# Three edits around the last layer's node stage: an earlier start for interleaved extra work, five norm groups ahead of the copies, and sums added on GpSimd

## The chip, the core and the metric

The kernel runs on one core of one Trainium2 chip. The metric is the device time of one execution in microseconds (us); for a kernel that was run several times it is the median.

## What is computed

Four graph layers over 3125 nodes with 128 features and 100,000 edges, all in fp32. Each layer is h = relu(layernorm(x)), x = x + layer(h). The layers are an edge MLP (with a residual of its own inside), a graph attention with 4 heads, a second attention with 8 heads and a bias, and a relational layer with 16 relations. Cut to the part at hand:

```python
h = relu(layernorm(x));  x = x + attention2(h, edges, W, a_left, a_right, bias)   # third layer
h = relu(layernorm(x))                                                            # fourth layer
weights = einsum('rb,bio->rio', coefficients, bases)      # 16 relation matrices
out = h @ w_self.T
out = out.at[src].add(h[dst] @ weights[edge_type])        # one term an edge
x = x + out
```

## The kernel before, in words

Nodes lie in 25 bins of 128 (the last one partly filled); a tile [128, 25, 128] holds x as `g.X`. Edges are sorted and cut into blocks of 512 (4 tiles of 128): 196 main blocks (numbers 0 to 195) and 12 extra ones (196 to 207), 208 in all; the extra blocks, and block 195, have 2 real tiles instead of 4. A stage is one hardware block: every engine runs its own instruction list, written out in full, and waits only where the text says `wait_ge`. Between stages all engines meet at a barrier.

**The attention stage** (`attention_sum`, third layer) goes over the 208 blocks in a software pipeline. GpSimd issues one gather DMA a tile (806 of them, line 1105, `att_row`). VectorE's list is made by `unrolled`: step k does `make_hot` of block k (L2352), `score` of block k-3 (L2362, waits for the gather), `message` of block k-4 (L2369, L2371) and `add_sum` of block k-6 (L1482, waits for TensorE's sum, L2340; TensorE starts the sum of block j once block j-2 is added and the message of j is there), and then takes one item of **extra work** with `next(extra, None)`. Steps run from 0 to 213; the extra work is taken from step `first` = `UNROLL` = 16 on, and what is left after step 213 runs behind the loop. The extra work is a chain of three generators: `add_bias` (9 items: the layer's bias into X), `merged_rows` (133 items: a merge sort of the edge words; its exchanges wait for DMAs that SyncE issues) and `relation_weights` (60 items of one 128x512 instruction, L360 and L366: the 16 relation matrices into `g.wall`), together 202 items.

**The relation stage** (`relation`, fourth layer) begins after the barrier. Its node part: the sums of the attention layer, divided by their denominators, are added to X; X is normed; H, its transpose `ht`, and 25 x 4 products of 128x512 (`product`, L1718) with `g.wall` make a table in HBM (`tables`, 25 writes of 1 MB, L1614). The norm (`Norm`) works in nine groups of three bins, `THREE`:

- VectorE: `residual` (L887: TMP = sums x 1/denominator, three instructions; L891: X += TMP, one 128x384 instruction), `scan` (bn_stats L897, bn_aggr L900), `scales` (L913, L914, waits for ScalarE's square root).
- ScalarE: `deviation` (L907, square root) and `apply` (L922, H, three instructions), put together in `scaled(n)`: deviation of group n, then apply of group n-1. Before the loop over bins it does `scaled(0)` to `scaled(2)`, with `keep_three` (L945, copies a transposed group from PSUM) after n = 1; then for each bin a: the copies of the bin's product banks into `stage` (L1672; from bin 4 on VectorE takes two of the four, L1810), and then `scaled(2a+3)`, `scaled(2a+4)` and, for a = 1, 4, 7..., `keep_three` of the next group.
- TensorE: `turn_three` (L937, transposes of a group) and the four products of a bin; product (a, part) waits until the copy of (a-1, part) has emptied its bank; bin 3n waits for `keep_three` of group n.
- SyncE: for each bin a write of `stage` to the table once the bin's copies are done; ahead of the writes of bins 1, 2 and 4 a third of H each to `tabh` (L1611), which wait for 3, 6 and 9 groups of `apply`. As the queue is in order, the last of them also waits for the copies of bin 3.
- GpSimd: waits for `s_node_i` and for the three writes to `tabh`; then 64 **early gathers** from `tabh` (L1640, 16 blocks), of which the last 16 (from block 12 on) go into the room of H and wait for the last transposes (`gp.wait_ge(s_t, len(THREE))`); then waits for all table writes; then the 742 gathers of the remaining 192 blocks (L1650), from the table into a ring of 16 blocks, which TensorE sums (L1756). Five output instructions on VectorE (L1876) and the writes of x end the kernel.

`TMP`, `acc` and `H` are free as homes of the early gathers once the norm is through.

Of the kernel before, what the change touches and what calls it, by code (L numbers as in the profile page):

```python
# [7 lines left out]
ALU = mybir.AluOpType  # L8
# [22 lines left out]
UNROLL = 16  # L31
# [815 lines left out]
def span(bins):  # L847

    return slice(bins[0], bins[-1] + 1)


class Norm:


    def __init__(self, nc, c, g, layer):
        self.g, self.layer = g, layer
        self.stats, self.mv = c.sb("stats", [P, N_BINS, 6]), c.sb("mv", [P, N_BINS, 2])
        self.eps = c.sb("eps", [P, 1])
        self.s_own, self.s_fin, self.s_var, self.s_std, self.s_rstd, self.s_h = (
            c.sem(n) for n in "own fin var std rstd h".split())  # L860

    def begin(self, v):

# [12 lines left out]
    def residual(self, v, n):  # L876

        g, ch, here = self.g, self.ch, span(THREE[n])
        if self.layer == 1:
            for a in THREE[n]:  # L880
                ins = v.scalar_tensor_tensor(g.X[:, a, :], g.bn2[:], g.acc[:, a, D:D + 1], g.X[:, a, :],
                                             ALU.mult, ALU.add)
            ch.do(ins)
            ch.do(v.tensor_tensor(g.X[:, here, :], g.X[:, here, :], g.acc[:, here, 0:D], ALU.add))
        else:
            for a in THREE[n]:
                ins = v.tensor_tensor(g.TMP[:, a, :].rearrange("p (h f) -> p h f", h=self.heads),  # L887
                                      self.sums[:, a, :, 0:self.f],
                                      self.den[:, a, :].unsqueeze(2).broadcast_to([P, self.heads, self.f]), ALU.mult)
            ch.do(ins)  # L890
            ch.do(v.tensor_tensor(g.X[:, here, :], g.X[:, here, :], g.TMP[:, here, :], ALU.add))  # L891
        v.sem_inc(self.s_fin, 1)

    def scan(self, v, n):

# [653 lines left out]
def relation(nc, g, args, tables, out):  # L1549
# [5 lines left out]
    with Core(nc, "rel") as c:  # L1555
        norm = Norm(nc, c, g, 3)
# [73 lines left out]

        @block.gpsimd
        def _(gp):
            gp.wait_ge(s_node_i, 1)
            gp.wait_ge(s_row, 48)
            for o in range(EARLY):
# [19 lines left out]
        def _(act):  # L1655
# [3 lines left out]
                if 0 < n <= len(THREE):  # L1659
                    norm.apply(act, n - 1)  # L1660

            for n in range(3):
                scaled(n)
                if n == 1:
                    keep_three(act, ht, p_t, 0, s_t, s_tc)
            for a in range(N_BINS):
                if a >= ring:
                    act.wait_ge(s_out[a % ring], 16 * (a // ring))
                for part in range(4):
                    if not by_vector(a, part):  # L1670
                        act.wait_ge(s_m, banks * a + part + 1)
                        act.copy(stage[:, a % ring, part * 512:(part + 1) * 512], p_m[part]).then_inc(s_ma, 1)  # L1672
                scaled(2 * a + 3)
                scaled(2 * a + 4)
                if a % 3 == 1 and a // 3 + 1 < len(THREE):
                    keep_three(act, ht, p_t, a // 3 + 1, s_t, s_tc)
            act.wait_ge(s_tabs, 1)
# [108 lines left out]
        def _(v):  # L1786
            ch = Chain(v, s_v)
            v.wait_ge(s_w, 1)
            v.tensor_copy(g.w_self[:], p_m[3][:, 0:D]).then_inc(s_wc, 1)
            norm.begin(v)  # L1790
            for n in range(len(THREE)):
                norm.residual(v, n)
                if n:
                    norm.scales(v, n - 1)
                norm.scan(v, n)
            norm.scales(v, len(THREE) - 1)
            v.wait_ge(s_word[0], 16)
            v.tensor_scalar(node_i[:], g.word[:, 0:EARLY * TILES], INDEX_BIT + 4, 0xFFF, ALU.logical_shift_right,
# [457 lines left out]
def attention_sum(nc, g, args):  # L2256
# [4 lines left out]
    with Core(nc, "att") as c:  # L2261
# [84 lines left out]
        def _(v):  # L2346
# [19 lines left out]
            def message(k, q, b):  # L2366
# [3 lines left out]
                for t in real_tiles(MIXED[k]):  # L2370
# [3 lines left out]

            unrolled([(0, make_hot), (3, score), (4, message),
                      (6, add_sum(nc, v, g, g.bin_d, p_sum, W, 2, s_sum, s_acc, s_tick))],
                     chain(add_bias(v, g), merged_rows(v, g, s_mrg, s_swap), relation_weights(v, g, s_in, s_wall)), UNROLL)


def graph_layers(nc, args, out):  # L2380
# [77 lines left out]
```

## Time and profile before

| | us |
|---|---|
| median of 3 runs | 4415.1 |
| lowest, highest run | 4408.89, 4421.24 |
| the profiled execution, its own time | 4400.82 |
| its span (first to last instruction) | 4399.1 |
| busy: PE, DVE, ACT, POOL | 3095.3, 2478.1, 1619.5, 3121.7 |

The profile is of one execution; all starts of rows are us from its span's start. PE is TensorE's matmuls, PEld its weight loads, DVE VectorE, ACT ScalarE, POOL GpSimd, SP SyncE; L1718 is line 1718 of the kernel before. A row of a timeline has start, length, engine, line, operation, written tile <- read tiles, shapes, xcount of like instructions that follow each other, and in brackets the idle time before it and what ended it. Neighbouring instructions of one engine overlap by a little, so the time that an instruction adds is the distance to the next start, not its length.

The attention stage's gathers run from 2302.80 to 3326.23, and its last VectorE instruction ends at 3339.69; the relation stage's node part runs from about 3340.6 to 3460; the 742 gathers from 3460.39 to about 4386.7.

### The profile page before, as it was taken

To read this page: it belongs to the slowest core of one execution; us is meant where nothing else is said; L and a number is where in the kernel's file an instruction comes from. 1 tells how busy PE (TensorE), PEld (TensorE's weight loads), DVE (VectorE), ACT (ScalarE), POOL (GpSimd) and SP (SyncE) were. 2 spreads that over 40 slices of the span, in tenths; PEclk is the share of its full clock that TensorE was granted. 3 is DMA by queue.
4 is the path that set the end of the run, shared out by engine and by line. 5 is a ranking of instruction groups with operands and counts; after the bars stand their busy time and mean duration, and the time that the engine had idled before them with its cause. 6 is when DMAs were issued, how large, how long until landed. Compare 5 with 4: busy or idle time off the path is not lost. (4 is left out here: it accounts for less than half of the span.)

```text
span 4399.1 us, 65956 instructions
## 1 busy us (share of the span) xinstructions
PE 3095.3 (70%) x17524; PEld 2307.5 (52%) x17524; DVE 2478.1 (56%) x8035; ACT 1619.5 (37%) x4881; POOL 3121.7 (71%) x3260
## 2 busy tenths in 40 slices
PE   4999999999335445444538989888987665555544
PEld 2555555555234344444528878787884333333333
DVE  6677777755437667666764666666666523333100
ACT  4333334334344445445541111111114433444332
POOL 4777777777477777777607777777773777777776
PEclk8999999999655555555555555555557878787655
DMA  4644444442334444444302222333224722222222
GB/s 98 144 95 93 93 95 92 95 91 36 89 103 107 106 106 112 103 108 110 71 29 57 66 70 75 84 79 89 61 57 168 174 53 53 53 53 53 53 53 62
DMA packets 422730, 372.66 MB, mean 85 GB/s; under 512 B 287296, under 2 KB 326090, under 8 KB 419035
## 3 DMA queue, kind: packets, MB, share of 16 engines
q0 software_dynamic: 103168, 178.48, 17.9%
q1 hardware_dynamic: 315736, 189.88, 16.7%
q8 instruction: 153, 2.51, 0.2%
q14 instruction: 217, 1.78, 0.1%
q10 hardware_dynamic: 3456, 0.01, 0.0%
HBM read 317.94 MB, written 35.47 MB: 80 GB/s over the span
## 5 line engine op out<-in xcount | busy, mean ns | idle before, releaser
L1105 POOL DMA_INDIRECT mlp_row<-tab,rec_d x806 | 782.7, 971 | 292.9 <-issue 238.4
L1105 POOL DMA_INDIRECT gat_row<-tab,rec_d x806 | 778.7, 966 | 265.3 <-issue 241.4
L1105 POOL DMA_INDIRECT att_row<-tab,rec_d x806 | 778.1, 965 | 255.7 <-issue 243.8
L1650 POOL DMA_INDIRECT rel_row<-tab,words_in x742 | 700.5, 944 | 226.1 <-issue 225.8
L2103 PE MATMUL gat_ps_sum<-gat_row,gat_hot 128*128 128x136 f32 x1612 | 407.1, 428 | 275.8 <-DVE gat_row L2174 251.2
L1756 PE MATMUL rel_ps_acc<-rel_row,rel_hot 128*128 128x128 f32 x1484 | 310.5, 373 | 402.1 <-DMA rel_row<-tab,words_in 377.8
L1756 PEld LDWEIGHTS rel_ps_acc<-rel_row,rel_hot 128*128 128x128 f32 x1484 | 264.6, 267 | 542.7 <-issue 542.7
L2340 PE MATMUL att_ps_sum<-att_row,att_hot 128*128 128x136 f32 x1612 | 432.2, 447 | 116.3 <-DVE acc L1482 112.4
L2103 PEld LDWEIGHTS gat_ps_sum<-gat_row,gat_hot 128*128 128x128 f32 x1612 | 351.0, 311 | 300.6 <-issue 264.5
L2340 PEld LDWEIGHTS att_ps_sum<-att_row,att_hot 128*128 128x128 f32 x1612 | 368.3, 324 | 190.9 <-DVE acc L1482 185.8
L1691 ACT ACTIVATE rel_hot<-iota,rel_local 128x128 f32<-128x128 f32 x806 | 257.8, 389 | 562.5 <-PE rel_ps_acc L1756 538.6
L2331 PEld LDWEIGHTS att_ps_t<-att_tgt,att_hot_t 128*128 128x128 f32 x1612 | 360.6, 324 | 0.2 <-ACT att_hot_t L2307 0.2
L2331 PE MATMUL att_ps_t<-att_tgt,att_hot_t 128*128 128x8 f32 x1612 | 334.5, 336 | 0.0
L2313 ACT ACTIVATE att_ps_wgt<-att_val 128x32 f32<-128x32 f32 (+1 forms) x208 | 41.6, 200 | 768.1 <-DVE att_row L2371 768.1
L2072 PE MATMUL gat_ps_t<-gat_tgt,gat_hot_t 128*128 128x12 bf16 x832 | 59.3, 181 | 305.4 <-DVE gat_raw L2137 289.5
L2022 ACT ACTIVATE gat_gap<-iota,rec_d 128x128 f32<-128x128 f32 x806 | 258.6, 395 | 0.0
L1482 DVE TENSOR_TENSOR acc<-acc,mlp_ps_sum 128x129 f32 x415 | 120.9, 291 | 241.9 <-PE mlp_ps_sum L1375 183.0
L1281 ACT ACTIVATE mlp_em<-mlp_ps_em,be 128x512 f32<-128x512 f32 (+1 forms) x208 | 140.3, 675 | 273.5 <-PE mlp_ps_em L1346 265.5
L1375 PEld LDWEIGHTS mlp_ps_sum<-mlp_nm,mlp_hot 128*128 128x128 f32 x1612 | 195.6, 190 | 83.6 <-issue 82.6
L1375 PE MATMUL mlp_ps_sum<-mlp_nm,mlp_hot 128*128 128x129 f32 x1612 | 235.4, 287 | 0.9 <-DVE mlp_nm L1430 0.9
L2072 PEld LDWEIGHTS gat_ps_t<-gat_tgt,gat_hot_t 128*128 128x128 bf16 x832 | 64.4, 120 | 324.3 <-DVE gat_raw L2137 296.2
L2322 PE MATMUL att_ps_hot<-ident,att_hot 128*128 128x128 f32 x806 | 214.1, 417 | 15.6 <-DVE att_hot L2352 15.5
(320 smaller groups left out, 5994.4 us busy)
## 6 DMA issues: line engine op xcount, KB each, us to landing
mlp_aim<-in_dst SPq DMA_DIRECT2D x195, 256.0 KB
gat_aim<-in_dst SPq DMA_DIRECT2D x195, 256.0 KB
tab<-rel_stage SPq DMA_DIRECT2D x25, 1024.0 KB, 4.2
mlp_row<-in_edge_attr SPq DMA_DIRECT2D x390, 64.0 KB
mlp_row<-tab,rec_d POOLq DMA_INDIRECT x806
gat_row<-tab,rec_d POOLq DMA_INDIRECT x806, 2.6
att_row<-tab,rec_d POOLq DMA_INDIRECT x806
rel_row<-tab,words_in POOLq DMA_INDIRECT x742, 2.5
```

Of the source, the lines that this page charges most:

```text
L1105: gp.indirect_dma_start(row[b][:, t, :], None, table, bass.IndirectOffsetOnAxis(offsets(order[k], t), axis=0)).then_inc(s_g[b], 16)
L1281: act.activation(by_half(em[b % 2])[:, :, 0:wide], p_em[:, :, 0:wide], ACT.Relu, bias=g.be2[:]).then_inc(s_emr, 1)
L1375: mm = pe.matmul(half_sum(p_sum, t // HALF_TILES, D + 1), hot[b % RING][:, t, :], nm[b % 2][:, t, :], start=(t % HALF_TILES == 0), stop=(t ...
L1650: gp.indirect_dma_start(row[r % UNROLL][:, t, :], None, tables, bass.IndirectOffsetOnAxis(g.index[:, at:at + 1], axis=0)).then_inc(s_g[r % ...
L1691: ins = act.activation(hot[k % HOTS][:, t, :], g.iota[:], ACT.Square, scale=-1.0, bias=local[:, at:at + 1])
L1756: mm = pe.matmul(p_acc[:, bass.ds(a * D, D)], hot[k % HOTS][:, t, :], here[:, t, :], start=False, stop=True, skip_group_check=True)
L2022: ins = act.activation(gap[b % 2][:, t, :], g.iota[:], ACT.Square, scale=-1.0, bias=g.rec_d[:, bass.ds(k * TILES + t, 1), 1].bitcast(F32))
L2072: mm = pe.matmul(p_t[:, at:at + 3 * H], hot_t[b % RING][:, here * P:(here + 1) * P], tgt[b][:, t // HALF_TILES, :], start=True, stop=True)
L2103: mm = pe.matmul(half_sum(p_sum[b % 2], t // HALF_TILES, ROW), hot[b % 4][:, t, :], rows[:, b, t, :], start=(t % HALF_TILES == 0), stop=(t ...
L2322: mm = pe.transpose(p_hot[b % 2][:, t * P:(t + 1) * P], hot[b][:, t, :], g.ident[:])
L2331: mm = pe.matmul(p_t[b % 2][:, t * T:(t + 1) * T], hot_t[b % 2][:, t * P:(t + 1) * P], tgt[b][:, t // HALF_TILES, :], start=True, stop=True)
L2340: mm = pe.matmul(half_sum(p_sum[b % 2], t // HALF_TILES, W), hot[b][:, t, :], flat[b][:, t, :], start=(t % HALF_TILES == 0), stop=(t % HAL ...
```

## The change

`unrolled` in `attention_sum` takes its first item of extra work at step 4 instead of 16. In the fourth layer `residual` ends after TMP is written (L887) and signals a new semaphore `s_shares`; the nine additions X += TMP are GpSimd's first instructions of the stage (`add_shares`), each signalling `s_fin`. VectorE does the multiplication of group n+1, waits for the addition of group n, scans group n, and only then does the scales of group n-1. ScalarE does `scaled(0)` to `scaled(4)` ahead of the copies, and `scaled(2a+5)`, `scaled(2a+6)` after those of bin a. In `Norm.residual` the new return is for layer 3 alone, so the other two attention node stages are as before.

```diff
@@ -856,8 +856,8 @@
         self.g, self.layer = g, layer
         self.stats, self.mv = c.sb("stats", [P, N_BINS, 6]), c.sb("mv", [P, N_BINS, 2])
         self.eps = c.sb("eps", [P, 1])
-        self.s_own, self.s_fin, self.s_var, self.s_std, self.s_rstd, self.s_h = (
-            c.sem(n) for n in "own fin var std rstd h".split())
+        self.s_own, self.s_fin, self.s_var, self.s_std, self.s_rstd, self.s_h, self.s_shares = (
+            c.sem(n) for n in "own fin var std rstd h shares".split())
 
     def begin(self, v):
 
@@ -887,9 +887,19 @@
                 ins = v.tensor_tensor(g.TMP[:, a, :].rearrange("p (h f) -> p h f", h=self.heads),
                                       self.sums[:, a, :, 0:self.f],
                                       self.den[:, a, :].unsqueeze(2).broadcast_to([P, self.heads, self.f]), ALU.mult)
+            if self.layer == 3:
+                ins.then_inc(self.s_shares, 1)
+                return
             ch.do(ins)
             ch.do(v.tensor_tensor(g.X[:, here, :], g.X[:, here, :], g.TMP[:, here, :], ALU.add))
         v.sem_inc(self.s_fin, 1)
+
+    def add_shares(self, gp):
+
+        for n, bins in enumerate(THREE):
+            there = self.g.X[:, span(bins), :]
+            gp.wait_ge(self.s_shares, n + 1)
+            gp.tensor_tensor(there, there, self.g.TMP[:, span(bins), :], ALU.add).then_inc(self.s_fin, 1)
 
     def scan(self, v, n):
 
@@ -1630,6 +1640,7 @@
 
         @block.gpsimd
         def _(gp):
+            norm.add_shares(gp)
             gp.wait_ge(s_node_i, 1)
             gp.wait_ge(s_row, 48)
             for o in range(EARLY):
@@ -1659,7 +1670,7 @@
                 if 0 < n <= len(THREE):
                     norm.apply(act, n - 1)
 
-            for n in range(3):
+            for n in range(5):
                 scaled(n)
                 if n == 1:
                     keep_three(act, ht, p_t, 0, s_t, s_tc)
@@ -1670,8 +1681,8 @@
                     if not by_vector(a, part):
                         act.wait_ge(s_m, banks * a + part + 1)
                         act.copy(stage[:, a % ring, part * 512:(part + 1) * 512], p_m[part]).then_inc(s_ma, 1)
-                scaled(2 * a + 3)
-                scaled(2 * a + 4)
+                scaled(2 * a + 5)
+                scaled(2 * a + 6)
                 if a % 3 == 1 and a // 3 + 1 < len(THREE):
                     keep_three(act, ht, p_t, a // 3 + 1, s_t, s_tc)
             act.wait_ge(s_tabs, 1)
@@ -1788,11 +1799,14 @@
             v.wait_ge(s_w, 1)
             v.tensor_copy(g.w_self[:], p_m[3][:, 0:D]).then_inc(s_wc, 1)
             norm.begin(v)
+            norm.residual(v, 0)
             for n in range(len(THREE)):
-                norm.residual(v, n)
+                if n + 1 < len(THREE):
+                    norm.residual(v, n + 1)
+                v.wait_ge(norm.s_fin, n + 1)
+                norm.scan(v, n)
                 if n:
                     norm.scales(v, n - 1)
-                norm.scan(v, n)
             norm.scales(v, len(THREE) - 1)
             v.wait_ge(s_word[0], 16)
             v.tensor_scalar(node_i[:], g.word[:, 0:EARLY * TILES], INDEX_BIT + 4, 0xFFF, ALU.logical_shift_right,
@@ -2374,7 +2388,7 @@
 
             unrolled([(0, make_hot), (3, score), (4, message),
                       (6, add_sum(nc, v, g, g.bin_d, p_sum, W, 2, s_sum, s_acc, s_tick))],
-                     chain(add_bias(v, g), merged_rows(v, g, s_mrg, s_swap), relation_weights(v, g, s_in, s_wall)), UNROLL)
+                     chain(add_bias(v, g), merged_rows(v, g, s_mrg, s_swap), relation_weights(v, g, s_in, s_wall)), 4)
 
 
 def graph_layers(nc, args, out):
```

## Rows read from the trace of the kernel before

**Rows 1.** The page, part 4: shares of the chain that ended last, by engine.
```profile
POOL 16%; issue 5%; PE 2%; DVE 0%; ACT 0%; DMA 0%; POOLq 0%; DVEq 0%
```

**Rows 2.** View of line 1650, the 742 gathers (ns min/median/max, first and last start).
```profile
L1650 POOL DMA_INDIRECT rel_row<-tab,words_in x742: 940/944/1261, 3460.4 to 4385.7; - x186
```

**Rows 3.** Timeline, VectorE, end of the attention stage (start us, us, engine line op, [idle before]).
```profile
3321.80 0.69 DVE L360 TENSOR_TENSOR att_part<-att_bases,att_coef 128x512 f32<-128x512 f32 x1
3322.40 0.68 DVE L2352 TENSOR_TENSOR att_hot<-att_ps_iota,rec_d 128x512 f32<-128x512 f32 x1
...
3329.98 0.17 DVE L2362 TENSOR_TENSOR att_val<-att_row,att_ps_t 128x16 f32<-128x16 f32 x1
...
3332.77 0.73 DVE L1482 TENSOR_TENSOR acc<-acc,att_ps_sum 128x136 f32 x2
...
3335.45 0.74 DVE L1482 TENSOR_TENSOR acc<-acc,att_ps_sum 128x136 f32 x2
3336.10 0.69 DVE L366 TENSOR_TENSOR wall<-wall,att_part 128x512 f32<-128x512 f32 x1
...
3339.00 0.69 DVE L366 TENSOR_TENSOR wall<-wall,att_part 128x512 f32<-128x512 f32 x1
```

**Rows 4.** Timeline, GpSimd: the attention stage's last gather.
```profile
3324.87 1.36 POOL L1105 DMA_INDIRECT att_row<-tab,rec_d  x1 [0.30 <-issue]
```

**Rows 5.** The page, part 6: a gather's time from issue to landing (last number, us).
```profile
gat_row<-tab,rec_d POOLq DMA_INDIRECT x806, 2.6
```

**Rows 6.** Timeline, TensorE: the last sum of the attention stage.
```profile
3333.56 1.28 PE L2340 MATMUL att_ps_sum<-att_row,att_hot 128*128 128x136 f32 x4 [0.45 <-DVE acc L1482]
```

**Rows 7.** Who waited for whom, VectorE, attention stage (us in total, times, longest us).
```profile
DVE att_val L2362 <- DMA att_row<-tab,rec_d: 300.5, 177, 4.0
```

**Rows 8.** Timeline, VectorE, the norm's first two groups of three bins.
```profile
3343.33 0.70 DVE L887 TENSOR_TENSOR TMP<-acc,den 128x128 f32<-128x128 f32 x3
...
3344.76 0.68 DVE L897 BATCH_NORM_STATS2 rel_stats<-X 128x6 f32<-128x128 f32 x3
...
3345.71 0.66 DVE L887 TENSOR_TENSOR TMP<-acc,den 128x128 f32<-128x128 f32 x3
...
3348.34 0.66 DVE L887 TENSOR_TENSOR TMP<-acc,den 128x128 f32<-128x128 f32 x3
```

**Rows 9.** Timeline, ScalarE, norm and copies of the first bins.
```profile
3348.66 1.25 ACT L922 ACTIVATE H<-X,mu,var 128x128 f32<-128x128 f32 x3
...
3353.60 0.58 ACT L1672 COPY rel_stage<-rel_ps_acc 128x512 f32<-128x512 f32 x1 [0.88 <-PE rel_ps_acc L1718]
...
3359.13 0.30 ACT L907 ACTIVATE std<-rel_mv,rel_eps 128x3 f32<-128x3 f32 x1 [0.23 <-DVE rel_mv L900]
...
3360.49 2.01 ACT L1672 COPY rel_stage<-rel_ps_acc 128x512 f32<-128x512 f32 x4
...
3370.70 2.03 ACT L1672 COPY rel_stage<-rel_ps_acc 128x512 f32<-128x512 f32 x4
```

**Rows 10.** Timeline, TensorE, products of the first bins.
```profile
3351.52 8.85 PE L1718 MATMUL rel_ps_acc<-wall,rec_d 128*128 128x512 f32 x16 [0.66 <-ACT rec_d L945]
...
3375.27 10.46 PE L1718 MATMUL rel_ps_acc<-wall,rec_d 128*128 128x512 f32 x24
```

**Rows 11.** Timeline, SyncE's queue: the last of three writes of H.
```profile
3373.15 0.41 SPq L1611 DMA_DIRECT2D tabh<-H  x1
```

**Rows 12.** Timeline, GpSimd: first of the 64 early gathers, the 49th, first of the 742.
```profile
3379.05 0.94 POOL L1640 DMA_INDIRECT TMP<-tabh,rel_node_i  x1 [52.82 <-DMA tabh<-H]
...
3440.43 0.94 POOL L1640 DMA_INDIRECT H<-tabh,rel_node_i  x1 [1.51 <-PE rel_ps_acc L937]
...
3460.39 0.94 POOL L1650 DMA_INDIRECT rel_row<-tab,words_in  x1 [0.30 <-issue]
```

**Rows 13.** Groups of instructions, GpSimd, shapes apart: the nearest to an add.
```profile
L929 POOL MEMSET acc<- 128x408 f32 x16 | 7.0, 438 | 116.2 <-DVEq L892 116.2
...
L178 POOL TENSOR_SCALAR_AFFINE_SELECT earlier<-ones 128x128 f32<-128x128 f32 x1 | 0.3, 292 | 0.1
```

## The prediction

> **What bounds the kernel now.** I read the page's chain shares first [rows 1]: they name almost only GpSimd, because the chain runs back gather by gather through the whole last stage. The view of line 1650 says why: 742 gathers from 3460.4 to 4385.7 at 0.944 us each [rows 2], which with the pause after each is (4385.7 - 3460.4) / 741 = 1.249 us a gather. Nothing in the change touches these gathers, their number or their pace, so the time can only move with the instant at which the first of them starts. That instant is reached through two stages, and each has to be read in its own timeline.
>
> The attention stage ends on VectorE, not on the gathers. VectorE waited 300.5 us in 177 pieces for gathers [rows 7], so in the middle GpSimd leads; but its last gather starts at 3324.87 [rows 4], and VectorE goes on to 3339.00 + 0.69 = 3339.69 [rows 3]. The last 3.6 us of that are five weight items (3336.10 to 3339.00 and its length), four of them behind the loop, with nothing else left to do.
>
> The node part ends where the first of the 742 starts, 3460.39 [rows 12]. Behind it stands the 49th early gather at 3440.43, which had waited 1.51 us for the last transposes; 16 gathers of 1.25 us follow. Those transposes are in TensorE's list after the products of bin 22, so what counts is how early TensorE gets through its products. From bin 5 on they run without a gap: 24 instructions, three bins, in 10.46 us, 3.44 us a bin without the transposes between [rows 10]. Before that, TensorE starts at 3351.52 and reaches bin 5 only at 3375.27: 23.75 us for five bins where 17.2 would do. So the norm and ScalarE's list are on the path only up to bin 4.
>
> **Part 1, extra work from step 4.** 202 items from step 16 leave 202 - 198 = 4 behind step 213; from step 4 they end with step 205, and steps 206 to 213 have none. An item adds 0.60 us in the loop (3321.80 to 3322.40) and (3339.00 - 3336.10) / 4 = 0.725 behind it [rows 3]. Removed from the end: 8 x 0.60 + 4 x 0.725 = 7.7 us. What is late next: the score of block 207 moves by four items from 3329.98 to 3327.6. It needs the last gather, 3324.87 plus 2.6 to landing [rows 5] is 3327.5, 3327.9 if this gather's 1.36 us instead of 0.944 counts too; so the landing just begins to bind. The addition of block 205 starts 5 items earlier, 3332.77 - 3.0 = 3329.8 [rows 3], that of 204 ends near 3329.4, and from there TensorE needs its two last sums, 1.28 us each [rows 6], to about 3332.0; the last addition (0.74) follows, to 3332.8. So **3339.7 becomes 3332.8, -6.9 us**; bounds -5.5 (landing 0.8 late and the sums in its tow) and -7.7. The 12 steps that now get items earlier, 4 to 15, pay nothing: VectorE waits there for gathers, up to 4.0 us a step and 300.5 / 177 = 1.7 on average [rows 7], against items like those of [rows 3], of 0.6, or twice that. The items' waits for the merge's DMAs move with them and keep their distance in steps.
>
> **Part 2, the sum on GpSimd.** VectorE's group cost 3348.34 - 3345.71 = 2.63 us [rows 8]. Multiplication and addition took 3344.76 - 3343.33 = 1.43 with their waits, the scan 3345.71 - 3344.76 = 0.95, so the scales 2.63 - 1.40 - 0.95 = 0.28. The addition and the wait for the multiplication go; the three multiplications alone add about 0.60. New pace: 0.60 + 0.95 + 0.28 = 1.83 us. The addition's price on GpSimd, 128x384 from two inputs, is in no row. Nearest below is the memset of 128x408, 0.438 (writes only); above, an affine select of 128x128 takes 0.292 with one input, three of them 0.88, and twice that for two inputs 1.75 [rows 13]. I take 1.0, nearer the select, since it reads too. Then GpSimd keeps pace with 1.83. The first group pays: its scan starts at 3344.03 + 1.0 + two handovers of 0.1 = 3345.2 instead of 3344.76. It gets this back, since the second scan now ends at 3345.2 + 0.95 + 0.60 + 0.95 = 3347.7, and scales 0 at 3348.0; ScalarE's first apply starts at about 3348.15 instead of 3348.66 [rows 9], TensorE's products at 3351.0 (2.86 later, as before). GpSimd has nothing else to do here: its first gather waited until 3379.05 [rows 12].
>
> The Trainium skill ("GPSIMD Engine Reference", section 3.1) measures an fp32 add of 2048 elements at 4497 ns; scaled to 384 that is an estimate of 0.84 us and a fixed part, and the sum would be the same to 0.2 us.
>
> **Part 3, five groups ahead.** ScalarE's list, with rows of before: a norm group 3360.49 - 3359.13 = 1.36, four copies 1.9 (2.01 long), keep_three 0.36 to 0.48 [rows 9]. keep_three ends at 3350.9, groups 1 to 3 take 4.1, so the copies of bin 0 begin at 3354.9, not 3353.60: 1.3 later, and that is hidden, because the fourth product of bin 0 ends 5.45 us after TensorE's start, the first 16 instructions being slow (8.85 us against 2 x 3.44 [rows 10]), at 3356.5. Copies of bin 0 end at 3357.0; two groups, 3359.7; bin 1, 3361.6; two groups and keep_three, 3364.7; bin 2, 3366.6; the last group is one bin, 0.4; the copies of bin 3 begin at **3367.0 against 3370.70** [rows 9]. TensorE starts bin 3 with the first free bank, 3365.3, bin 4 at 3368.8, and after the transposes bin 5 at 3372.6 instead of 3375.27 [rows 10]: **-2.7 us**, and from there all moves alike. Check of the other two arms: the last write of H (3373.15 [rows 11]) stands on SyncE's queue behind bin 3's table write, whose copies now end 3.3 earlier; early gathers start at 3375.8, the 48th is through at 3435.7, and the last transposes come at 3437.4, so the wait at the 49th stays the one that binds and grows from 1.5 to 1.7 us. Table writes land 8 us ahead of need before and after. Bounds: at 1.75 for the addition the pace is 1.95, products start 0.3 later than before and the copies of bin 0 at 3356.5, -1.5; at 0.44 it is -3.2.
>
> **Sum.** -6.9 - 2.7 = -9.6 us. The profiled execution took 4400.8 (span 4399.1 and 1.7 around it); changed, 4391.2. It lies 14.3 below the median shown, so on the median: 4415.1 - 9.6 = **4405.5**.
>
> **Rivals.**
> - *GpSimd and VectorE take turns.* If an addition and VectorE's instructions exclude each other, a group costs 1.83 + 1.0 = 2.83, above the 2.63 of before; the fourth apply ends 4 x 1.0 later, minus the 0.2 of slack, and part 3 turns from -2.7 to +1.1: 4409.3. For it speaks that gathers on GpSimd are stretched in places, 1.36 against 0.944 [rows 2, 4]; against it that all but the multiplications and the small scale product have one input tensor. Chance 0.1.
> The Trainium skill ("SBUF — State Buffer", section "Who interferes with whom") states this for a VectorE instruction with two SBUF inputs beside a GpSimd instruction that reads SBUF: the later one waits out the other. Here that would hit the multiplications of the second group beside the first addition, 0.3 to 0.6 us once, and the later additions lie beside the scans; by this narrower rule the sum is -9.2. No row of before shows the pair.
> - *The end of attention is bound elsewhere.* If the landing or TensorE's sums hold the end, only the items behind the loop and one or two more go, -4: total -6.7, 4408.4. Chance 0.15.
> - *Node part unmoved.* Something other than TensorE's early bins sets the last transposes, part 3 gives nothing and the change does only the half of what it says: -6.9, 4408.2. The gap of 23.75 against 17.2 speaks against. Chance 0.1.
> - *Slower: the copies starve.* ScalarE now stands before the copies of bin 0 until group 4 is scanned and group 3 applied; all four product banks are full behind it, TensorE stops, and each us of it goes to the end. With GpSimd's pace c setting the groups, the copies begin at 3346.9 + 5c. The gain is eaten when that is 9.8 after 3354.9, c = 3.6; slower by 0.3% (13.2 us) it is from c = 6.2, six times my price and above every bound from rows. Chance 0.03.
> - *More than forecast*, -12 or beyond, from gathers no longer stretched and a cold start of TensorE shorter than before: 4402. Chance 0.07.
> The forecast keeps 0.55.
>
> **Range and chances.** What a measurement of this kernel can tell from no change is about 0.3%, 13.2 us: 4401.9 to 4428.3. All cases but the last two fall between 4402 and 4410; the runs of before spread over 12.3 us, so a median may sit 5 us off. Range 4395 to 4416. Faster by over 0.3% needs -13.2: the upper case and the scatter below the forecast, 0.22; slower 0.03; within, 0.75.
>
> **What the profile of the changed kernel would show.** VectorE's last instruction before the barrier is an addition (L1482's), about 5.3 us after the last gather landed (12.2 before), and no weight item within the last eight steps. GpSimd's nine additions stand in the timeline at about 1.0 us each and the groups on VectorE at 1.83; above 2.6 part 2 is wrong. Products start 0.5 us sooner from the barrier, bin 5 comes 21.6 us after the first product instead of 23.75, and the 49th early gather still waits for the transposes. The 742 gathers keep 1.249 us. The prediction is wrong if the barrier does not move by 5.5 us or more, or if the distance from the barrier to the first of the 742 does not shrink by 1.5 or more.

## The result, and the profile after

| | before | changed |
|---|---|---|
| median, us | 4410.53 (9 runs) | 4403.21 (9 runs) |
| lowest, highest | 4406.19, 4421.24 | 4397.97, 4408.41 |
| span of the profiled execution | 4399.1 | 4399.0 |
| last gather of attention to TensorE's first instruction of the relation stage | 15.77 | 9.53 |
| from there to the first of the 742 gathers | 119.75 | 117.73 |

The changed kernel takes 0.9983 of the time, 95% interval 0.9975 to 0.9992: 7.3 us less by the medians, 3.5 to 11 by the interval. The forecast was -9.6 us and 4405.5; with the median of before now at 4410.53 it would have read 4400.9. That 4403.21 lies so near to 4405.5 is in part luck: the median that the forecast started from was 4.6 us too high, and the gain that it took off was 2.3 us too large. The change is real and lies inside 0.3%.

The two profiled executions have the same span, which needs an explanation before anything else is read from them. The views of the gather line tell it (nanoseconds minimum/median/maximum, then first and last start). Before:

```profile
L1105 POOL DMA_INDIRECT mlp_row<-tab,rec_d x806: 940/944/3096, 63.1 to 1090.3; - x162
...
L1105 POOL DMA_INDIRECT att_row<-tab,rec_d x806: 940/944/1717, 2302.8 to 3324.9; - x162
```

Changed:

```profile
L1115 POOL DMA_INDIRECT mlp_row<-tab,rec_d x806: 941/947/4114, 62.8 to 1091.9; - x162
...
L1115 POOL DMA_INDIRECT att_row<-tab,rec_d x806: 941/947/1717, 2306.8 to 3331.4; - x162
```

The median gather is 0.947 us in the changed kernel's profile and 0.944 before, in the edge MLP too, a stage that the change does not touch. The attention stage began 4.0 us later (2306.8 against 2302.8), its 806 gathers took 1024.6 instead of 1022.1 us, and the 742 took (4385.6 - 3458.6) 927.0 instead of 925.3:

```profile
L1661 POOL DMA_INDIRECT rel_row<-tab,words_in x742: 941/947/1196, 3458.6 to 4385.6; - x186
```

4.0 + 2.5 + 1.7 = 8.2 us against the change, and 6.24 + 2.02 = 8.3 us for it, so the spans agree. The 2.5 and the 1.7 are the pace (806 x 0.003 is 2.4, 742 x 0.003 is 2.2). The 4.0 ahead of the stage can't be put down to it: e7 and e8, at 0.944, began the stage at 2306.8 and 2306.4 as well. In the experiments the pace goes with the chip and not with the kernel: e1 and e10, the same code, had 0.947 on one chip and 0.944 on another. On which chips the two profiles above were taken is not known. The profiled execution of before is also faster than all nine runs in the table, by 9.7 us against their median; 3224 gathers at 0.003 us more would make just that (an estimate), which suggests, but does not show, that those runs went at 0.947. So what the change did is read from distances inside the stages, and the time from the medians.

**The end of attention.** VectorE, timeline:

```profile
3326.24 0.68 DVE L2366 TENSOR_TENSOR att_hot<-att_ps_iota,rec_d 128x512 f32<-128x512 f32 x1
...
3328.93 0.18 DVE L2376 TENSOR_TENSOR att_val<-att_row,att_ps_t 128x16 f32<-128x16 f32 x1 [0.29 <-DMA att_row<-tab,rec_d]
...
3331.47 0.18 DVE L2376 TENSOR_TENSOR att_val<-att_row,att_ps_t 128x16 f32<-128x16 f32 x1 [0.73 <-DMA att_row<-tab,rec_d]
...
3334.12 0.18 DVE L2376 TENSOR_TENSOR att_val<-att_row,att_ps_t 128x16 f32<-128x16 f32 x1 [0.83 <-DMA att_row<-tab,rec_d]
...
3337.91 0.74 DVE L1492 TENSOR_TENSOR acc<-acc,att_ps_sum 128x136 f32 x2 [0.57 <-DVE acc L1492]
3339.22 0.73 DVE L1492 TENSOR_TENSOR acc<-acc,att_ps_sum 128x136 f32 x2 [0.57 <-PE att_ps_sum L2354]
```

TensorE, timeline:

```profile
3335.98 2.69 PE L2354 MATMUL att_ps_sum<-att_row,att_hot 128*128 128x136 f32 x8 [1.37 <-DVE acc L1492]
3340.91 0.45 PE L1718 MATMUL rel_ps_acc<-ident,w_self 128*128 128x128 f32 x1 [2.24 <-PEq L145]
```

GpSimd, timeline, the last attention gather, two of the nine additions, and the three gathers that answer to [rows 12]:

```profile
3331.38 0.95 POOL L1115 DMA_INDIRECT att_row<-tab,rec_d  x1 [0.30 <-issue]
3344.37 1.17 POOL L902 TENSOR_TENSOR X<-X,TMP 128x384 f32<-128x384 f32 x1 [12.04 <-DVE TMP L887]
3345.76 0.99 POOL L902 TENSOR_TENSOR X<-X,TMP 128x384 f32<-128x384 f32 x1 [0.23 <-DVE TMP L887]
...
3376.84 0.97 POOL L1651 DMA_INDIRECT TMP<-tabh,rel_node_i  x1 [17.56 <-DMA tabh<-H]
...
3438.64 0.95 POOL L1651 DMA_INDIRECT H<-tabh,rel_node_i  x1 [2.07 <-PE rel_ps_acc L947]
...
3458.64 0.95 POOL L1661 DMA_INDIRECT rel_row<-tab,words_in  x1 [0.30 <-issue]
```

No weight item stands in the last steps, and the last addition (3339.22 + 0.73 = 3339.95) is VectorE's last work, where [rows 3] had five items from 3336.10 on. VectorE now waits for the gathers in the last three scores, for 0.29, 0.73 and 0.83 us: the landing binds.

**The node part.** VectorE, ScalarE and TensorE, timelines:

```profile
3343.59 2.10 DVE L887 TENSOR_TENSOR TMP<-acc,den 128x128 f32<-128x128 f32 x6
3345.61 0.67 DVE L907 BATCH_NORM_STATS2 rel_stats<-X 128x6 f32<-128x128 f32 x3
...
3347.23 0.67 DVE L907 BATCH_NORM_STATS2 rel_stats<-X 128x6 f32<-128x128 f32 x3
...
3349.03 0.67 DVE L907 BATCH_NORM_STATS2 rel_stats<-X 128x6 f32<-128x128 f32 x3
```

```profile
3355.20 1.04 ACT L1683 COPY rel_stage<-rel_ps_acc 128x512 f32<-128x512 f32 x2
...
3367.78 1.08 ACT L1683 COPY rel_stage<-rel_ps_acc 128x512 f32<-128x512 f32 x2
```

```profile
3351.41 9.33 PE L1729 MATMUL rel_ps_acc<-wall,rec_d 128*128 128x512 f32 x16 [0.66 <-ACT rec_d L955]
...
3361.24 3.67 PE L1729 MATMUL rel_ps_acc<-wall,rec_d 128*128 128x512 f32 x8 [0.16 <-ACT rel_stage L1683]
3366.21 7.11 PE L1729 MATMUL rel_ps_acc<-wall,rec_d 128*128 128x512 f32 x16 [1.30 <-ACT rel_stage L1683]
...
3373.48 7.03 PE L1729 MATMUL rel_ps_acc<-wall,rec_d 128*128 128x512 f32 x16
```

The scans stand 1.80 us apart (3347.23, 3349.03) instead of 2.63 [rows 8]. The copies of bin 3 begin 26.87 us after TensorE's first instruction (3367.78 - 3340.91) instead of 30.06, bin 5's products 32.57 instead of 34.63 [rows 10], the early gathers 35.93 instead of 38.41, and the 49th waits 2.07 us for the last transposes instead of 1.51 [rows 12].

### The profile page after: what moved, and what is told of

Its sections match the earlier page's. It is cut to its first block and busy times, and to the rows that moved or that the text cites. A ratio compares the mean times of both kernels' runs of the same rounds, so it can differ in the third digit from the quotient of the medians.

```text
span 4399.0 us, 65947 instructions
## 1 busy us (share of the span) xinstructions
PE 3087.6 (70%) x17524; PEld 2302.7 (52%) x17524; DVE 2467.3 (56%) x8026; ACT 1620.1 (37%) x4881; POOL 3136.4 (71%) x3269
```

## The experiments

Each experiment is a kernel of its own. The times of e5 to e8 and of e12 are of a single execution each; the others are medians of 11 or 12. Executions of one kernel spread over 10 to 24 us here, so single times are given but prove nothing, and the distances, read from one profiled execution each, carry the argument. "Tail" is the distance from the start of attention's last gather to TensorE's first instruction of the relation stage, "node" that from there to the first of the 742 gathers. e5 to e8 ran together, on one chip, where the kernel before took 4405.2. e1 to e4 ran together on another chip, e9 to e12 later on the chip of e5 to e8. In both of these sessions transfers were slower (attention's 806 gathers took about 1180 us from first to last instead of 1022, at the same median gather) and the kernel before took 5197.4 and 5199.9; those are called the slow-memory sessions here, and their numbers are compared only with each other.

### e5: the additions on GpSimd, three groups ahead

```diff
-            for n in range(5):
+            for n in range(3):
                 scaled(n)
-                scaled(2 * a + 5)
-                scaled(2 * a + 6)
+                scaled(2 * a + 3)
+                scaled(2 * a + 4)
```
and the extra work from `UNROLL`.

> The kernel before with only the additions on GpSimd (and VectorE's new order), three groups ahead of the copies. Theory (the node part is bound by ScalarE's list from bin 0 on, so both edits are needed): VectorE's group at 1.80 us instead of 2.63; from TensorE's first instruction to the first of the 742 gathers 118 to 119.5 us, since ScalarE no longer waits for VectorE's scans but still stands between the bins. Rival (VectorE's pace was the whole limit): 117.7, as in the changed kernel. Rival (first addition and second multiplications in each other's way cost more than the pace brings): 119.75 or more.

Measured: 4401.94 us, beside 4405.16; node 118.34, tail 15.77. VectorE's scans of two groups:

```profile
3351.10 0.67 DVE L907 BATCH_NORM_STATS2 rel_stats<-X 128x6 f32<-128x128 f32 x3
...
3352.90 0.67 DVE L907 BATCH_NORM_STATS2 rel_stats<-X 128x6 f32<-128x128 f32 x3
```

1.80 us apart, as in the changed kernel. How much of the node part's gain this edit is has to be read with care, since the distance scatters with the first 16 product instructions: with the norm of before it was 119.75 where they took 8.85 us (before) and 120.32 where they took 9.42 (e8). Like with like, e5 (8.77) is 1.4 us under before (8.85), and the changed kernel (9.33) is 2.6 under e8 (9.42). So the additions alone give a little over half, and VectorE's pace was not the only limit.

### e6: five groups ahead, additions on VectorE

```diff
-            for n in range(3):
+            for n in range(5):
                 scaled(n)
-                scaled(2 * a + 3)
-                scaled(2 * a + 4)
+                scaled(2 * a + 5)
+                scaled(2 * a + 6)
```

> The kernel before with only the five groups ahead, additions on VectorE. Theory: VectorE's group stays at 2.63, the fourth apply must wait for the fifth scan, which ends 2 us after the place where ScalarE wants it; the copies of bin 0 begin at least 4 us later than before (3358 against 3353.6), TensorE stops at bin 1, and the distance to the first of the 742 gathers is 119.5 to 122 us, so this edit alone gains nothing or loses. Rival (the order of ScalarE's list alone makes the gain): 117.7.

Measured: 4403.4 us, beside 4405.16; node 120.38, and tail 14.79, though this kernel's end of attention is that of before (15.77): the tail scatters by up to 1 us on one code. Part of that has a visible cause: among the gathers that start in the stage's last 20 us of gathers, five took 1.33 to 1.46 us in e6 and three took 1.36 to 1.38 in before, so e6's last gather starts later for the same end (what stretches them is shown in the last section). ScalarE's timeline, two square roots that wait for VectorE and the first copies:

```profile
3355.71 0.30 ACT L907 ACTIVATE std<-rel_mv,rel_eps 128x3 f32<-128x3 f32 x1 [0.99 <-DVE rel_mv L900]
...
3358.33 0.30 ACT L907 ACTIVATE std<-rel_mv,rel_eps 128x3 f32<-128x3 f32 x1 [1.18 <-DVE rel_mv L900]
...
3359.69 1.52 ACT L1672 COPY rel_stage<-rel_ps_acc 128x512 f32<-128x512 f32 x3
```

The square roots wait 0.99 and 1.18 us for VectorE (bracket), 2.62 apart, and the first copies begin 17.05 us after TensorE's first instruction instead of 12.96. The edit alone gains nothing; the two edits need each other, as expected.

### e7: three more additions a group

```diff
             gp.wait_ge(self.s_shares, n + 1)
+            for i in range(3):
+                self.slow.do(gp.tensor_tensor(self.spare[:, i, 0:len(bins), :], there, self.g.TMP[:, span(bins), :], ALU.add))
             gp.tensor_tensor(there, there, ...
```

> The changed kernel with three further additions of 128x384 on GpSimd ahead of each group's own, into room that nothing reads; each waits for the one before. GpSimd's pace becomes 4 x 1.0 + 0.5 = 4.6 us a group. Theory (the prediction's slower rival: the copies of bin 0 wait for the fifth sum, and each us of delay goes to the end): the copies of bin 0 begin about 29 us after TensorE's first instruction instead of 14.3, and the first of the 742 gathers 130 to 133 us after it instead of 117.7. Rival (other slack takes up the delay): under 125. On exclusion: if VectorE's instructions with two SBUF inputs (L887, 3 x 0.2 us) and GpSimd's additions shut each other out, L887's mean length rises well above its 0.276 us while bn_stats (one input) keeps 0.281.

Measured: 4416.08 us, beside 4405.16; node 135.41, above the expected 130 to 133; first copies 28.34 us after TensorE's first instruction, where 29 was expected. The pace of the groups came out at 4.31 us. So the slower rival of the prediction is a real mechanism: 14.05 us of delay at the first copies cost 17.7 at the gathers. It is more than one for one mainly because the later groups come late too: TensorE waited 5.54, 2.75 and 1.67 us at bins 1, 2 and 3, against 0, 0.16 and 1.30 in the changed kernel. Another 0.7 us is bin 1 itself, whose eight products took 5.54 us after that wait, at a granted clock of 0.50 in the first 2 us (3.67 at bin 2). It did not decide here, since the addition costs 1.0.

The groups of VectorE's instructions in the node part (busy us, mean ns, then idle) show who shuts out whom, in e7:

```profile
L887 DVE TENSOR_TENSOR TMP<-acc,den 128x128 f32<-128x128 f32 x25 | 11.3, 503 | 0.0
L926 DVE SCALAR_TENSOR_TENSOR mu<-rel_mv,var 128x3 f32<-128x3 f32 x8 | 5.8, 730 | 0.3
L909 DVE BATCH_NORM_STATS2 rel_stats<-X 128x6 f32<-128x128 f32 x25 | 5.7, 283 | 12.0 <-POOL X L904 12.0
```

and in the changed kernel:

```profile
L887 DVE TENSOR_TENSOR TMP<-acc,den 128x128 f32<-128x128 f32 x25 | 6.6, 319 | 0.0
L907 DVE BATCH_NORM_STATS2 rel_stats<-X 128x6 f32<-128x128 f32 x25 | 5.7, 278 | 0.0
```

The multiplication (two inputs in SBUF) takes 503 ns on average in e7, 319 in the changed kernel, and took 277 in the same stretch of before. The small product of the scales, two inputs as well, goes to 730 ns; in the changed kernel it took 163. bn_stats, with one input, keeps 278 to 283 throughout, beside the same additions. GpSimd's own additions take 1.12 to 1.13 us where a multiplication stands beside them, and 0.99 to 1.00 elsewhere. This is the rule of the Trainium skill ("SBUF — State Buffer", section "Who interferes with whom"), that an instruction of VectorE with two SBUF inputs and one of GpSimd that reads SBUF exclude each other. By that rule, the trace agrees in which instructions are hit; each group of three multiplications and each small product loses 0.7 to 0.8 us, less than one addition of 1.0.

### e8: the extra work from step 10

```diff
-                     chain(add_bias(v, g), ...), UNROLL)
+                     chain(add_bias(v, g), ...), 10)
```

> The kernel before with the extra work begun at step 10: items end with step 211, so two steps of the last are free of them and none is left behind the loop. Theory: 4 x 0.725 us from behind the loop and about 2 x 0.60 in it, no wait for the landing yet: from the last gather to TensorE's first instruction 15.8 - 4.1 = 11.7 us. Rival (only the items behind the loop count, the landing binds the rest): 12.9, and then the start at step 4 would not have given more than 3.

Measured: 4400.64 us, beside 4405.16; tail 11.13. VectorE's timeline:

```profile
3335.89 0.69 DVE L366 TENSOR_TENSOR wall<-wall,att_part 128x512 f32<-128x512 f32 x1
3336.58 0.73 DVE L1482 TENSOR_TENSOR acc<-acc,att_ps_sum 128x136 f32 x2
3337.89 0.74 DVE L1482 TENSOR_TENSOR acc<-acc,att_ps_sum 128x136 f32 x2 [0.58 <-DVE acc L1482]
```

The last item (3335.89) now stands between additions, and the last addition waits 0.58 us as in the changed kernel. 4.64 us of the tail are gone with six steps, 6.24 with twelve. The four items behind the loop are 2.9 of that and the two in it 1.2, 4.1 in all as expected; the other 0.5 is within the 1 us by which the tail scatters. The six items more that step 4 takes away are worth 1.6 together, not 3.6: there the landing and the last sums hold the end.

The tail can't show what the earlier items cost in the first steps. Measured over the whole stage, from the first gather to TensorE's first instruction, this kernel needs 1033.2 us, e7 (step 4) 1033.3, and the kernels with step 16 need 1037.8 (before), 1038.0 (e5) and 1037.4 (e6), all at a median gather of 0.944. So the 1.6 us of tail between step 10 and step 4 are not seen in the whole stage; the changed kernel's own 1034.1 at 0.947 a gather is 1031.7 when 806 x 0.003 is taken off. The starts of the gathers tell where e7 loses them: the 151st gather starts 188.1 to 188.4 us after the first in before, e5, e6 and e8, and 189.55 after it in e7, where the 150 gathers ahead of it were busy 143.5 us instead of 142.0 to 142.4. In the changed kernel it starts after 189.12 us, 188.67 with the pace (150 x 0.003) taken off. From there to the last gather all six take the same within 0.8 us, the pace again taken off. So the items at steps 4 to 15 cost 0.3 to 1.5 us through longer gathers in the first blocks; how much of that range is scatter stays open.

### e4, e1, e2, e10, e11: the parts, timed, with slow memory

e4 is the changed kernel again; e1 and e10 are the kernel before with

```diff
-                     chain(add_bias(v, g), ...), UNROLL)
+                     chain(add_bias(v, g), ...), 4)
```

and e2 and e11 the changed kernel without it.

> The changed kernel once more, beside the others. Both distances as in its first profile, 9.5 and 117.7 us, within 0.4 each, while the span may differ by 5 us either way through the pace of the gathers alone (median gather 0.944 in the profile of before, 0.947 in that of after). Time: 7 us less than before, within 3.

> The kernel before with only the start of the extra work at step 4. Theory (two parts add up): the distance from the start of the attention stage's last gather to TensorE's first instruction of the relation stage is 15.8 us before and 9.5 in the changed kernel; here 9.5 too, and from TensorE's first instruction to the first of the 742 gathers the 119.75 us of before, within 0.3. Time: 6 us less than before. Rival (the shorter node part feeds on the earlier extra work, for instance by a warmer start): the second distance would shrink here as well, to 118 or so. Rival (the extra work only moves and lengthens the gathers of the first blocks): the 806 gathers of attention would take 2 us or more longer than before at an equal median gather.

> The changed kernel with the extra work begun at step 16 as before. Theory: the end of attention as before (15.8 us from the last gather to TensorE's first instruction), the node part as in the changed kernel (117.7 us from there to the first of the 742 gathers, against 119.75). Time: 2 us less than before, which 5 rounds can hardly tell from nothing. Rival (the node part gives nothing of its own): 119.7.

> The kernel before with only the start of the extra work at step 4, for the two distances on a chip of the usual pace. Theory: from the last gather of attention to TensorE's first instruction 9.5 us against 15.8, node part 119.8 to 120.3 (the slow first products vary by 0.6), time 6.2 us less than before, nearly all of the changed kernel's gain. Rival (the node edits carry the gain): within 3 us of before.

> The changed kernel with the extra work begun at step 16. Theory: 15.8 us from the last gather to TensorE's first instruction, node part 117.1 to 117.7 us, time 2 to 2.6 us less than before. Rival (it gives nothing): ratio at 1.000, node part 119.8.

| kernel | ratio, 95% interval | tail | node |
|---|---|---|---|
| e4 changed | 0.9981 (0.9972 to 0.9989) | 40.70 | 162.25 |
| e1 step 4 alone | 0.9981 (0.9972 to 0.9990) | 41.24 | 165.75 |
| e10 step 4 alone | 0.9990 (0.9980 to 0.9999) | 40.60 | 164.73 |
| e2 node edits alone | 0.9995 (0.9985 to 1.0006) | 46.61 | 162.32 |
| e11 node edits alone | 1.0000 (0.9991 to 1.0010) | 47.63 | 161.33 |

The expected absolute distances are all missed, since they were those of fast memory. The differences hold. Tail: the three kernels with step 4 have 40.85 on average, the two without 47.12, 6.3 us apart, as with fast memory (6.24). Node: the two with the old norm 165.24, the three with the new one 161.97, 3.3 us apart against 2.0. By time, the gain of the changed kernel (-10.7 us by the medians, a little more than the 7 within 3 expected) is that of step 4, 5 to 10 us in the ratios; the node edits alone (-2.6 and -3.6 us by the medians) can't be told from nothing by time, and e4 is no faster than e1. Only the distance shows them. Over the whole stage the three kernels with step 4 need 1222.3 us on average and the two without 1227.1, 4.8 apart. The rival of e1, gathers longer by 2 us or more, is not borne out but leaves a trace: from the first gather to the last, e1 took 1.2 us more than e2 and e10 1.6 more than e11. Nothing suggests that step 4 and the node edits need or hinder each other. e1 and e10 are the same code: the median gather was 0.947 on the chip of e1 to e4 and 0.944 on that of e5 to e12.

### e3, e9, e12: transposes and the last write of H earlier

```diff
+TURNED = {1: 1, 4: 2, 5: 3, 6: 4, 7: 5, 8: 6, 9: 7, 10: 8}
-                if a in (1, 2, 4):
-                    n = (1, 2, 4).index(a)
+                if a in (1, 2, 3):
+                    n = (1, 2, 3).index(a)
-                if a % 3 == 1 and a // 3 + 1 < len(THREE):
-                    turn_three(pe, g, norm, p_t, a // 3 + 1, s_tc, s_t)
+                if a in TURNED:
+                    turn_three(pe, g, norm, p_t, TURNED[a], s_tc, s_t)
```
with `keep_three` alike. e12 leaves SyncE's order as it was.

> The changed kernel with two further edits: the transposes of groups 2 to 8 follow bins 4 to 10 instead of 4, 7, ... 22, and the third write of H stands on SyncE's queue ahead of the table write of bin 3 instead of bin 4. Theory (the last transposes and, close behind, SyncE's order hold back the early gathers): the wait at the 49th early gather, 2.07 us in the changed kernel, goes to nothing; the first early gather starts 3 us sooner, and the first of the 742 follows it by 64 x 1.25 = 80 us: 113 us after TensorE's first instruction against 117.7. The table writes, 4.2 us to landing, are still 3 us ahead. Time: 4 to 5 us less than the changed kernel, 11 to 13 less than before. Rival (the table writes or ScalarE's list, which now has a transposed group in each of seven bins, takes over): products end later than before and the distance stays at 116 or above.

> The kernel of e3 again, since e3 ran on a chip whose memory moved slowly, where every table write was late and TensorE stood still for 40 us beside the early gathers. Theory, if the table writes land in 4.2 us again: the 49th early gather no longer waits, the first early gather starts 33.4 us after TensorE's first instruction (as in e3, before its chip's stall) instead of 35.9, and the first of the 742 follows at 33.4 + 80 = 113.4 instead of 117.7: 4.3 us under the changed kernel, 12 under the one before. Rival (the early gathers, now 2.5 us nearer to the first table writes, slow those, and products end late): 116 or more.

> The kernel of e9 without its second edit: the third write of H stands behind the table write of bin 3 as in the changed kernel. Theory (two limits close behind each other): the early gathers start at 35.5 to 36 us as in the changed kernel and run through without the wait of 2.07 us, so the first of the 742 comes at 115.6 to 116 us after TensorE's first instruction, between 117.7 and 113.4. Rival (the wait for the transposes was never a limit, another wait stands at the same place): 117.7.

Measured, all three with slow memory: e3 ratio 0.9980 (0.9971 to 0.9989), node 164.03; e9 0.9983 (0.9974 to 0.9992), node 166.59; e12, one execution, 5196.76 us beside 5199.94, node 179.76. The first early gather did start sooner, after 33.37 and 32.50 us in e3 and e9 against 35.54 in e4, and the 49th came at 100.97 and 100.15 instead of 142.24. In e12 the first started after 36.38 and the 49th after 99.70. The time did not follow: e3 took 5184.75 us beside e4's 5186.64, e9 5192.61 beside e10's 5192.87. Here the table writes crawl while early gathers run; the gathers themselves keep 1.25 us each. Two windows of the node part of e4 (us; busy time and count of each engine, granted clock, DMA share, GB/s), the first with early gathers running, the second while GpSimd waits for the transposes:

```profile
4004.00:4030.00 26.00, 8.27 (x8) 2.01 (x8) 1.56 (x4) 1.37 (x3) 19.60 (x21) 0.50 0.32 101
4056.00:4082.00 26.00, 26.00 (x66) 11.61 (x65) 10.97 (x19) 9.43 (x17) 0.00 (x0) 1.00 0.69 283
```

and one of the changed kernel with fast memory, with both:

```profile
3407.00:3433.00 26.00, 26.00 (x66) 11.47 (x65) 10.97 (x19) 9.35 (x17) 19.72 (x21) 1.00 0.90 338
```

101 GB/s with both at once, 283 with the writes alone, 338 with fast memory and both. So what was a wait of 2 us at the 49th gather is one of 47 us here, and it lets the writes catch up. With the transposes early that wait shrinks to 7.9 us in e3, 8.0 in e9 and 3.7 in e12 (nothing was expected), the remaining 16 gathers go on into the stall, and GpSimd waits for the table instead, 43.3 us in e3. GpSimd's waits in e9 and e12 (us in total, times, longest):

```profile
POOL rel_row L1662 <- DMA tab<-rel_stage: 46.8, 1, 46.8
```

```profile
POOL rel_row L1662 <- DMA tab<-rel_stage: 60.4, 1, 60.4
```

The first rival (table writes take over) is what these sessions showed. Whether the edit gives its 4 us where memory is fast was not seen: the question stays open, and no kernel here is shown to beat the changed one.

## Why the prediction was right, point by point

- **What bounds the kernel.** Right. The 742 gathers keep their number and, at an equal median gather, their pace: 925.3 to 925.7 us in before, e5, e6, e7 and e8.
- **Part 1, -6.9 us.** The tail gave -6.24 (6.3 with slow memory; 5.3 against e6's), more than the 5.5 below which the prediction called itself wrong. Up to the last score it went as written: 2.74 us after the last gather's start (3334.12 - 3331.38) where 3327.6 - 3324.87 = 2.7 was forecast, and the landing binds. The term that was too small is the handover from TensorE's last sum to the addition: the sums ended at 3335.98 + 2.69 = 3338.67 and the addition began at 3339.22, 0.55 us later, where the sum put 0.1. That is 0.45 of the 0.66 us; the two sums took 2.69 where 2 x 1.28 stood, 0.1 more. The rival "bound elsewhere" had its condition come true, since landing and sums do hold the end, but not its price of -4.
- **The cover of the first 12 steps.** Put at nothing, and not quite right: by the 151st gather the earlier items had cost 0.3 to 1.5 us in longer gathers. Over the whole stage the gain is 4.4 us in e7, 6.0 in the changed kernel at equal pace (1033.3 and 1031.7 against 1037.7, the mean with step 16) and 4.8 with slow memory. By that measure part 1 is 1 to 2.5 us under the forecast, and whether it reaches those 5.5 us stays open.
- **Part 2, the addition at 1.0 us.** Right: 0.99 to 1.00, and VectorE's pace 1.80 for 1.83. The first addition took 1.17 and the six multiplications beside it 2.10 instead of about 1.3, so the first scan stood 2.02 us after the first multiplication, not 1.87; the products started 10.50 us after TensorE's first instruction instead of 10.88, -0.38 for -0.5. This is the narrow form of the "take turns" rival, at 0.15 us on the path where 0.3 to 0.6 was put; its wide form, all instructions excluding each other, is refuted by bn_stats in e7.
- **Part 3, -2.7 us.** Measured -2.02. The copies of bin 0 began at 14.29, forecast 14.26 (3354.9 - 3340.64); those of bin 3 at 26.87 for 26.4. Of the missing 0.7, 0.5 is the first 16 product instructions: 9.33 us where 8.85 stood in the working. That is not the change's: e5 had 8.77 and e8, with the node part of before, 9.42, and its node distance was 120.32 for 119.75. The working took one execution's value for a constant. Against e8, which had the same slow start, the gain is 2.6 us, so the mechanism and nearly all of its size hold.
- **The other arms.** Right: the wait at the 49th gather stayed the binding one and grew, to 2.07 us where 1.7 was forecast; the table was in time. The early gathers started 35.93 us after TensorE's first instruction where the working has 35.2 (3375.8 - 3340.64): bin 3's copies took 2.7 us instead of 1.9, since ScalarE now waited for TensorE between them.
- **The slower rival** has its mechanism shown and its price: break-even had been put at a pace of 3.6 us a group, which makes 4.31 slower by 5 x 0.71 = 3.6 us; e7 was 10.9 us slower than before, so the price was put too low. By the slope of 17.7 us for 14.05 at the first copies, break-even lies below 3.6 (an estimate from two kernels, no run stands there; the 10.9 is of single executions, and the distances give 9.5).
- **The total.** -6.9 - 2.7 = -9.6 against 8.3 in the distances and 7.3 in the medians; the missed terms were small and on the same side: a handover at 0.1 us, a slow start at the value of one execution, and earlier items at nothing. The stated range, 4395 to 4416, would have held the median of before too; it is the distances, not the time, that bear the mechanism out.

## What to carry to other kernels

Work that is spread over the steps of a loop should end some steps before the loop does: here eight steps free of items and none behind it took 4.4 to 6 us off a stage of 1037, while the landing of the last gather set where further room stopped paying. Handing an elementwise step to GpSimd paid in full only together with a longer lead on the next engine (e5 -1.4, e6 nothing, both -2.0 to -2.6), and the instructions beside it on VectorE had mostly one input; e7 shows what those with two pay. When the effect sought is a few microseconds in 4400, read it as distances between events inside a stage: pace and scatter moved the span by 8.2 us, as much as the change did.

## What the runs showed of the hardware that was not expected

- The same gather code ran at a median of 0.947 us on one chip (one session) and 0.944 on another (two sessions); over the 3224 gathers of the kernel that is near 10 us of GpSimd's time.
- Gathers are stretched by VectorE instructions with two SBUF inputs. Two pairs from the changed kernel, in each the gather starts 0.13 us behind the VectorE instruction:

```profile
3320.39 0.68 DVE L360 TENSOR_TENSOR att_part<-att_bases,att_coef 128x512 f32<-128x512 f32 x1
3320.52 1.38 POOL L1115 DMA_INDIRECT att_row<-tab,rec_d  x1 [0.30 <-issue]
...
3326.24 0.68 DVE L2366 TENSOR_TENSOR att_hot<-att_ps_iota,rec_d 128x512 f32<-128x512 f32 x1
3326.37 0.94 POOL L1115 DMA_INDIRECT att_row<-tab,rec_d  x1 [0.30 <-issue]
```

  In the last 35 us of attention's gathers in before, the changed kernel, e6 and e8, every gather that starts 0.04 to 0.17 us behind the start of a weight item (L360 or L366, both inputs in SBUF) takes 1.33 to 1.46 us, and one that starts 0.34 to 0.43 behind it takes 1.07 to 1.16. Gathers at the same distance behind `make_hot` or `add_sum`, which have one input in PSUM, take 0.94 or 0.95. So a weight item that falls on the start of a gather costs up to 0.5 us of GpSimd's time.
- TensorE's first 16 product instructions come after a wait of 8.2 to 8.6 us. They took 9.33 and 9.42 us (changed kernel, e8) where the granted clock stood at 0.50, the 1.2 GHz level, through their first 4 us, and 8.85 and 8.77 (before, e5) where it had begun to rise within them (0.56 and 0.58 on average); each 8 later take 3.44 us at 1.0. In e7 it was back at 0.50 after a wait of 5.54 us.
- One chip ran the kernel before at 4405 us in one session and at 5200 in a later one, with the same granted clock (0.70 in all profiles) and the same length of copies on ScalarE (586 to 588 ns); the loss is in transfers, 101 GB/s for table writes and gathers together against 338. What slowed them is not known.
- A VectorE instruction of 128x3 elements with two inputs rose from 0.16 to 0.73 us beside back-to-back GpSimd additions (e7).
